# The row maxima take the position bias from SBUF in a combined VectorE instruction

## The chip, the cores and the metric

The kernel runs on one core of a Trainium2 chip. The metric is the device time of one launch in microseconds (us), the median of several runs. An engine named here is one of the core's five: PE is TensorE (matrix products; PEld is its weight load), DVE is VectorE, ACT is ScalarE, POOL is GpSimd, SP is SyncE, which here only issues transfers.

## What is computed

A transformer block over 32 batches of 512 rows of 256 features, with a modulation per batch:

```python
mod = (_silu(L0_c) @ L0_wmod).reshape(L0_c.shape[0], 6, 1, -1)
h = _layernorm(x, axis=-1) * (1 + ca) + sa
x = x + ga * attention(h)
h = _layernorm(x, axis=-1) * (1 + cb) + sb
x = x + gb * ffn(h)
```

The attention has 16 heads of 16 features. Its scores get a bias that depends on the head and on the distance of query and key alone, in 32 buckets that are full beyond a distance of 64 and are constant for keys ahead of the query:

```python
scores = jnp.einsum('bhqd,bhkd->bhqk', q * scale, k)
scores = scores + position_bias * 8.0
attn = softmax(scores)
```

The feed-forward part quantizes its input, its weights and its hidden values (704 wide) to a 4-bit format in blocks of 16, with products in full precision between them.

## The kernel before, in words

**Setup** (to about 98 us of the span) loads and quantizes the weights and builds the bias tables. Then a software pipeline runs over the batches, `for n` from -2 to 32, of which 4 to 29 are a hardware loop over pairs of iterations. An iteration has 16 steps `s` of four places `j`; four steps are a tile of 128 rows of the output, so that an iteration has 4 tiles and 64 places. Each engine has its own program, written out by hand in that same order, and engines meet at semaphores. A table (`JOBS`) says at which place TensorE makes which product of the projections, of the output projection and of the feed-forward part; they use two PSUM banks in turn (`ps_x`), so a job waits until the reader of the job two before it has read.

**Scores** are made twice. `scores` (L593 to L596) makes them with keys on the partitions, for ScalarE to take the exponential of two heads at once (L790) and for `weigh` (L630) to sum the values with. The softmax needs the maximum of each row first, and it has to be there before these scores are made, since it is subtracted through an additional row of `q_rows`. So `maxima` (L609 to L612), one iteration ahead, makes the scores with queries on the partitions, 128 queries by 512 keys in a PSUM bank, and `reduce_max` on VectorE (L1018) takes the negated maximum over the keys into `neg_max`. There is one such pair at each place: 64 in a batch, 2048 in all. The two engines share three PSUM banks for it (`RING_M`): TensorE may write the bank for maximum m once VectorE has read m - 3.

**The bias.** Constant parts of it ride in rows of `q_rows` and `k_rows`. What is left is a band around the diagonal. It is added on TensorE by a second matmul into the same bank, of the reversing matrix `rev` with `band_m` (in fp16): 192 columns wide, or 128 for the first query block (j = 0), which is one in four. `scores` adds its own band in the same manner from `band_t` (L594, L596).

**VectorE** also has, between these maxima, the low parts of high and low splits (`low_of`, L1063; `low_of_hidden`, L1071), the residual sums (`add_attention`, L1083 and L1086; `add_ffn`), statistics and scales (L1094 to L1105, `block_scales` L1053 to L1057), the activation (`silu_times_up`, L1115 and L1121) and the division by the softmax sum (L1047). Its queue is in order: whatever stands ahead of a maximum delays the bank that TensorE waits for. In a tile the places are written (r, j), with r = s mod 4. The activation of the third chunk of the hidden values stands at (2, 3), `block_scales` of 704 values behind the maximum of (3, 0), and the low part of the context, `ctx_l`, ahead of the maximum of (0, 1); ScalarE must first have copied its high part `ctx_h` (L863), and TensorE waits for `ctx_l` with the output projection at (0, 3).

After 32 maxima TensorE transposes them (L680), ScalarE copies them as bf16 into `max_rows` (L858), and a transfer puts them in place in `q_rows`.

## Time and profile before

| | |
|---|---|
| runs | 3733.33, 3735.27, 3738.55 us; median 3735.27 |
| the profiled execution | 3743.46 us, its span 3741.6 us |
| busy in the span | PE 3432.3 (92%), PEld 2016.3 (54%), DVE 2807.5 (75%), ACT 2128.2 (57%), POOL 1711.9 (46%) us |
| mean granted TensorE clock | 0.974 of full speed |
| transfers | mean 63 GB/s, 31.4% of the 16 DMA engines' time |
| the chain that ended last | PE 69%, ACT 10%, issue 7%, DVE 5%, DMA 4% of the span |

Times in the profile are us unless ns is written; an instruction that starts before the one ahead of it has ended overlaps it in the pipeline, so what an instruction costs its engine is the distance of two starts and not its duration. "[0.54 <-PE ...]" at a row's end is idle time of the engine ahead of it and what ended it.

### The profile page before, as it was taken

Reading aid. Unit: us, or ns where it says so; the run is one execution under the profiler, and the core shown is the slowest. Engines: PE = TensorE matmul, PEld = TensorE weight load, DVE = VectorE, ACT = ScalarE, POOL = GpSimd, SP = SyncE. Lnnn points to the kernel's source line nnn. Section 1 sums busy time; section 2 is a strip of 40 time slices with the busy share of each in tenths; the row PEclk is TensorE's granted clock in tenths of the full one; section 3 lists DMA queues with packets and bytes.
Section 4 is the critical chain, followed back from the end, with each engine's and each line's share of the span. In section 5 each row is a group of like instructions: output and inputs, shape, how many; then the busy total and the mean of one; then the engine's idle time right before and its main releaser. Section 6 shows DMA issues by size and latency. Waiting matters only on the chain.

```text
span 3741.6 us, 78263 instructions
## 1 busy us (share of the span) xinstructions
PE 3432.3 (92%) x22910; PEld 2016.3 (54%) x22910; DVE 2807.5 (75%) x5866; ACT 2128.2 (57%) x3352; POOL 1711.9 (46%) x2095
## 2 busy tenths in 40 slices
PE   2599999999999999999999999999999999999986
PEld 1245555555555555555555555555555555555555
DVE  7457877777777777777777777777777877777854
ACT  2256666655666555566655556656556566555552
POOL 2214444444544445454444544444445444444454
PEclk6799999999999999999999999999999999999997
DMA  3553232333323233332323332332333232333000
GB/s 98 84 95 71 52 66 56 60 74 74 69 57 67 48 70 74 73 64 63 64 45 73 76 73 57 61 63 55 73 76 73 51 68 56 61 73 69 18 22 12
DMA packets 199173, 236.95 MB, mean 63 GB/s; under 512 B 23552, under 2 KB 177568, under 8 KB 198736
## 3 DMA queue, kind: packets, MB, share of 16 engines
q1 hardware_dynamic: 198736, 231.51, 31.4%
q8 instruction: 228, 3.74, 0.4%
q14 instruction: 209, 1.71, 0.2%
HBM read 163.59 MB, written 67.31 MB: 62 GB/s over the span
## 4 chain that ended last, share of the span: by engine, by line
PE 69%; ACT 10%; issue 7%; DVE 5%; DMA 4%; SPq 3%; ACTq 1%; POOL 1%; DVEq 0%; POOLq 0%
PE ps_x L641 21%; PE ps_o L630 10%; PE rings L593 10%; PE rings L609 9%; PE ps_x L667 6%; ACT probs L790 5%; DMA x_in<-in_x 3%; PE rings L612 3%; PE rings L594 2%; PE ps_x L674 2%; SPq L484 2%; ACT magic L818 2%; PE rings L596 2%; PE ps_x L706 1%; PE ps_x L685 1%
## 5 line engine op out<-in xcount | busy, mean ns | idle before, releaser
L1018 DVE TENSOR_REDUCE neg_max<-rings 128x1 f32<-128x512 f32 x2048 | 1369.2, 680 | 292.4 <-PE rings L612 265.7
L790 ACT ACTIVATE probs<-rings 128x1024 f32<-128x1024 f32 x1024 | 1050.1, 1025 | 767.7 <-PE rings L596 759.2
L609 PE MATMUL rings<-k_rows,q_rows 120*128 120x512 bf16 x2048 | 779.7, 386 | 24.0 <-DVE neg_max L1018 12.5
L593 PE MATMUL rings<-q_rows,k_rows 121*128 121x512 bf16 x2048 | 727.9, 383 | 73.3 <-ACT probs L790 50.3
L630 PE MATMUL ps_o<-probs,values 128*32 128x512 f32 x4096 | 549.5, 609 | 0.9 <-ACT probs L790 0.9
L612 PE MATMUL rings<-band_m,rev 128*128 128x192 f16 (+1 forms) x2048 | 494.6, 241 | 0.0
L609 PEld LDWEIGHTS rings<-k_rows,q_rows 120*128 120x128 bf16 x2048 | 197.6, 96 | 516.0 <-DVE neg_max L1018 308.4
L594 PE MATMUL rings<-band_t,rev 128*128 128x128 f16 x2048 | 450.4, 220 | 0.0
L1282 POOL TENSOR_TENSOR hidden<-hidden,inv 128x704 f32<-128x704 f32 x128 | 178.6, 1395 | 556.2 <-DVE inv L1057 556.2
L596 PE MATMUL rings<-band_t,rev 128*128 128x128 f16 (+1 forms) x2048 | 431.3, 211 | 0.0
L596 PEld LDWEIGHTS rings<-band_t,rev 128*128 128x128 f16 x2048 | 201.3, 98 | 246.8 <-issue 1.5
L641 PE MATMUL ps_x<-w_gu_h,xq_h 128*128 128x512 f32 (+1 forms) x768 | 323.9, 422 | 10.0 <-DVE hq_l L1071 7.8
L1253 POOL TENSOR_TENSOR hidden<-hidden,magic 128x704 f32<-128x704 f32 x128 | 195.2, 1525 | 281.4 <-ACT magic L820 281.4
L1115 DVE SCALAR_TENSOR_TENSOR tanh<-tanh,ps_x 128x256 f32<-128x256 f32 (+1 forms) x384 | 152.0, 396 | 226.7 <-ACT tanh L877 222.3
L593 PEld LDWEIGHTS rings<-q_rows,k_rows 121*128 121x128 bf16 x2048 | 197.5, 96 | 197.4 <-ACT probs L790 90.2
L641 PE MATMUL ps_x<-w_gu_h,xq_l 128*128 128x512 f32 (+1 forms) x768 | 293.9, 383 | 0.0
L641 PE MATMUL ps_x<-w_gu_l,xq_h 128*128 128x512 f32 (+1 forms) x768 | 291.6, 380 | 0.0
L877 ACT ACTIVATE tanh<-ps_x 128x256 f32<-128x256 f32 (+1 forms) x384 | 138.7, 361 | 197.7 <-PE ps_x L641 197.7
L1063 DVE TENSOR_TENSOR ctx_l<-ps_x,ctx_h 128x256 fp32r<-128x256 f32 x128 | 54.4, 425 | 240.5 <-ACT ctx_h L863 238.9
L641 PE MATMUL ps_x<-w_dn_h,hq_h 128*128 128x256 f32 x768 | 230.2, 300 | 1.5 <-DVE hq_l L1071 1.5
L641 PE MATMUL ps_x<-w_dn_l,hq_h 128*128 128x256 f32 x768 | 219.6, 286 | 0.0
L641 PE MATMUL ps_x<-w_dn_h,hq_l 128*128 128x256 f32 x768 | 219.2, 285 | 0.0
(191 smaller groups left out, 6889.9 us busy)
## 6 DMA issues: line engine op xcount, KB each, us to landing
parts_dram<-parts SPq DMA_DIRECT2D x128, 384.0 KB, 2.3
q_rows<-parts_dram SPq DMA_DIRECT2D x384, 128.0 KB, 4.3
k_rows<-parts_dram SPq DMA_DIRECT2D x384, 128.0 KB, 6.9
mod_rows<-mod_rows_dram SPq DMA_DIRECT2D x32, 640.0 KB, 5.0
x_in<-in_x SPq DMA_DIRECT2D x32, 512.0 KB, 8.7
x_mid<-in_x SPq DMA_DIRECT2D x128, 128.0 KB, 2.1
out<-x_mid SPq DMA_DIRECT2D x128, 128.0 KB, 1.7
probs<-in_wmod SPq DMA_DIRECT2D x1, 1536.0 KB, 7.5
```

What stands on the lines that cost most here:

```text
L593: mm(ps_s[:, bank, :], kr[0:ROW_MAX + 1, h, k0:k0 + P], qr[0:ROW_MAX + 1, h, :], start=True, stop=False)
L594: mm(ps_s[:, bank, k0:k0 + P], rev[:, 0, :], band_t[:, h, :], start=False, stop=False)
L596: mm(ps_s[:, bank, k0 + HALF:k0 + HALF + w], rev[:, 1, :], band_t[:, h, 0:w], start=False, stop=True).then_inc(scores_ready, 1)
L609: mm(ps_m[:, bank, :], q_rows[par][0:ROW_MAX, h, j * P:(j + 1) * P], k_rows[par][0:ROW_MAX, h, :], start=True, stop=False)
L612: mm(ps_m[:, bank, k0:j * P + P], rev[:, 2, :], band_m[:, h, c0:], start=False, stop=True).then_inc(mscores_ready, 1)
L630: m = mm(ps_o[32 * j:32 * j + 32, :], values[:, par, kb, h * VW:h * VW + 32], prob(u, j), start=kb == 0, stop=kb == NT - 1)
L641: m = mm(out, left[a][:, dt, :], right[b][:, dt, columns], start=i == 0, stop=i == len(terms) - 1)
L667: m = mm(ps[:, :], w[:, dt, half * P:(half + 1) * P], h_t[:, dt, :], start=dt == 0, stop=dt == DT - 1)
L790: A(prob_pair(s, j), ps_s, ACT.Exp).then_inc(exp_done, 1)
L1018: v.tensor_reduce(neg_max[:, par, 4 * h + j:4 * h + j + 1], ps_m[:, (4 * h + j) % RING_M, :], AX.X, ALU.max, negate=True).then_inc(max_don ...
L1253: q.tensor_tensor(hid, hid, magic3[:], ALU.add).then_inc(f3_pool.sem, 1)
L1282: q.tensor_tensor(blocks(hid), blocks(hid), spread(inv3[:], FF // BLK), ALU.mult).then_inc(f2_pool.sem, 1)
```

## The change

Five things are different.

- `maxima` on TensorE makes the product of queries and keys alone. The matmul with `band_m` is gone.
- `reduce_max` on VectorE issues a memset of one column, which now carries the wait for TensorE, and then one `tensor_tensor_reduce`: the bank plus 512 columns of `band_z` from SBUF, written back into the bank, with the maximum of the sums in `row_max`. The compiler makes two instructions of it: the pass over 512 columns, and one that writes out the maximum (both print as ISA below).
- `band_z` is a table of fp16, `[128, 320 + 16 x 576]`, zero but for the band of each head; for query block j the instruction reads 512 columns from a start that is 128 j columns further to the left, so that the band comes to lie on the diagonal.
- The setup fills it: a memset of the table, a cast of the Hankel matrix to fp16 into memory that is free then, 8 matmuls of two heads with `rev`, and 16 casts from PSUM, two for each matmul.
- The maximum is no longer negated by VectorE. The ScalarE copy of 32 rows multiplies by -1. The scratch memory for descriptors of the GpSimd DMA is made smaller, for room.

```diff
-        band_m = sb("band_m", [P, H, 3 * HALF], F16)
+        band_z = sb("band_z", [P, 5 * HALF + H * 9 * HALF], F16)
...
+            pe.wait_ge(su_dve, SD["hank"])
+            for i in range(H // 2):
+                if i >= 3:
+                    pe.wait_ge(su_dve, SD["hank"] + 2 * (i - 2))
+                mm(setup_a[:, i % 3, 0:6 * HALF], rev[:, 2, :], hank2_half[:, 2 * i:2 * i + 2, :],
+                   start=True, stop=True).then_inc(su_pe, 1)
...
                 mm(ps_m[:, bank, :], q_rows[par][0:ROW_MAX, h, j * P:(j + 1) * P], k_rows[par][0:ROW_MAX, h, :],
-                   start=True, stop=False)
-                k0, c0 = (0, HALF) if j == 0 else (j * P - HALF, 0)
-                mm(ps_m[:, bank, k0:j * P + P], rev[:, 2, :], band_m[:, h, c0:], start=False,
-                   stop=True).then_inc(mscores_ready, 1)
+                   start=True, stop=True).then_inc(mscores_ready, 1)
...
-                                i = A(max_rows[:], ps[0:32, 0:P], ACT.Copy).then_inc(m_act.sem, 1)
+                                i = A(max_rows[:], ps[0:32, 0:P], ACT.Identity, scale=-1.0).then_inc(m_act.sem, 1)
...
-            step(v.tensor_copy(band_m[:], hank2))
-            step(v.memset(band_m[HALF:P, :, 2 * HALF:3 * HALF], 0.0))
-            step(v.memset(band_m[0:HALF, :, 0:HALF], 0.0))
+            step(v.memset(band_z[:], 0.0))
             dve.wait_ge(su_pe, SP_["wT"])
+            step(v.tensor_copy(hank2_half, hank2))
+            mark("hank")
+            for i in range(H // 2):
+                dve.wait_ge(su_pe, SP_["wT"] + i + 1)
+                rows = setup_a[:, i % 3, 0:6 * HALF].rearrange("p (h n) -> p h n", h=2)
+                heads = slice(2 * i, 2 * i + 2)
+                step(v.tensor_copy(band_m[0:HALF, heads, 0:2 * HALF], rows[0:HALF, :, 0:2 * HALF]))
+                step(v.tensor_copy(band_m[HALF:P, heads, HALF:3 * HALF], rows[HALF:P, :, HALF:3 * HALF]))
...
-                v.tensor_reduce(neg_max[:, par, 4 * h + j:4 * h + j + 1], ps_m[:, (4 * h + j) % RING_M, :], AX.X, ALU.max,
-                                negate=True).then_inc(max_done, 1)
+                v.memset(wait_pad[:, 1 + 4 * h + j:2 + 4 * h + j], 0.0)
+                ps, bias = ps_m[:, (4 * h + j) % RING_M, :], 9 * HALF * h + (6 - 2 * j) * HALF
+                v.tensor_tensor_reduce(ps, ps, band_z[:, bias:bias + S], 1.0, LOWEST, ALU.add, ALU.max,
+                                       row_max[:, par, 4 * h + j:4 * h + j + 1]).then_inc(max_done, 1)
```

On VectorE, from the maximum of (2, 3) to the second instruction behind that of (3, 1), in the part ahead of the hardware loop. Before (`hidden` is the activation, `scale` and `inv` its block scales):

```order
L1121 SCALAR_TENSOR_TENSOR hidden<-tanh,ps_x 128x192
L1018 TENSOR_REDUCE neg_max<-rings 128x1 x2
L1053 TENSOR_REDUCE scale<-hidden 128x44
L1055 TENSOR_SCALAR scale<-scale 128x44
L1057 RECIPROCAL inv<-scale 128x44
L1018 TENSOR_REDUCE neg_max<-rings 128x1
L1103 SCALAR_TENSOR_TENSOR ffn_in<-magic,ffn_in 128x256
L1105 SCALAR_TENSOR_TENSOR ffn_in<-magic,ffn_in 128x256
```

The same stretch now:

```order
L1136 SCALAR_TENSOR_TENSOR hidden<-tanh,ps_x 128x192
L1031 MEMSET wait_pad 128x1
L1033 ISA rings,row_max<-rings,band_z 128x512
L1033 ISA row_max 128x1
L1031 MEMSET wait_pad 128x1
L1033 ISA rings,row_max<-rings,band_z 128x512
L1033 ISA row_max 128x1
L1068 TENSOR_REDUCE scale<-hidden 128x44
L1070 TENSOR_SCALAR scale<-scale 128x44
L1072 RECIPROCAL inv<-scale 128x44
```

Each maximum is three instructions in the place of one; nothing else has moved.

On TensorE at (3, 0) and (3, 1): the maximum's product, the product with the values, the next maximum's product, and the feed-forward part's last product. Before:

```order
L609 MATMUL rings<-k_rows,q_rows 128x512
L612 MATMUL rings<-band_m,rev 128x128
L630 MATMUL ps_o<-probs,values 32x512 x4
L609 MATMUL rings<-k_rows,q_rows 128x512
L612 MATMUL rings<-band_m,rev 128x192
L641 MATMUL ps_x<-w_dn_h,hq_h 128x256
```

Now (rows on semaphores left as they stand):

```order
L619 MATMUL rings<-k_rows,q_rows 128x512
L637 MATMUL ps_o<-probs,values 32x512 x4
L124 REGISTER_ALU
L619 MATMUL rings<-k_rows,q_rows 128x512
L124 ISA x2
L648 MATMUL ps_x<-w_dn_h,hq_h 128x256
```

The band's matmul is gone from behind each product, and the order of the others is the same.

## Rows read from the trace of the kernel before

**Rows 1.** The page's first part: busy time and share of each engine.

```profile
PE 3432.3 (92%) x22910; PEld 2016.3 (54%) x22910; DVE 2807.5 (75%) x5866; ACT 2128.2 (57%) x3352; POOL 1711.9 (46%) x2095
```

**Rows 2.** The page's costliest groups: the maxima on the two engines.

```profile
L1018 DVE TENSOR_REDUCE neg_max<-rings 128x1 f32<-128x512 f32 x2048 | 1369.2, 680 | 292.4 <-PE rings L612 265.7
...
L609 PE MATMUL rings<-k_rows,q_rows 120*128 120x512 bf16 x2048 | 779.7, 386 | 24.0 <-DVE neg_max L1018 12.5
...
L612 PE MATMUL rings<-band_m,rev 128*128 128x192 f16 (+1 forms) x2048 | 494.6, 241 | 0.0
```

**Rows 3.** Busy time in the four tiles of one steady iteration, from `ctx_l` to `ctx_l`.

```profile
core 0: us, PE busy (x) PEld busy (x) DVE busy (x) ACT busy (x) POOL busy (x), PEclk, DMA share, GB/s
1705.90:1734.26 28.36, 27.89 (x187) 16.10 (x184) 21.34 (x43) 19.54 (x33) 12.75 (x18) 1.00 0.05 15
1734.26:1761.61 27.35, 26.37 (x174) 15.07 (x174) 20.92 (x43) 16.69 (x27) 15.17 (x18) 1.00 0.54 113
1761.61:1786.49 24.88, 23.52 (x170) 14.00 (x171) 20.47 (x43) 14.49 (x24) 13.96 (x17) 1.00 0.14 49
1786.49:1814.68 28.19, 27.19 (x187) 16.79 (x185) 21.67 (x52) 14.86 (x24) 11.13 (x16) 1.00 0.52 84
sum 108.78, PE 104.97 PEld 61.95 DVE 84.40 ACT 65.57 POOL 53.01; mean PE 26.24 PEld 15.49 DVE 21.10 ACT 16.39 POOL 13.25
```

**Rows 4.** TensorE's timeline: the band's matmul and what starts behind it.

```profile
1771.67 0.22 PE L612 MATMUL rings<-band_m,rev 128*128 128x128 f16 x1
1771.73 0.39 PE L706 MATMUL ps_x<-ident,hidden 128*128 128x128 f32 x2
...
1775.86 0.39 PE L609 MATMUL rings<-k_rows,q_rows 120*128 120x512 bf16 x1
1776.09 0.25 PE L612 MATMUL rings<-band_m,rev 128*128 128x192 f16 x1
1776.18 0.38 PE L593 MATMUL rings<-q_rows,k_rows 121*128 121x512 bf16 x1
```

**Rows 5.** VectorE's timeline where the first batch's maxima run alone.

```profile
168.04 7.26 DVE L1018 TENSOR_REDUCE neg_max<-rings 128x1 f32<-128x512 f32 x12 [1.33 <-PE rings L612]
```

**Rows 6.** VectorE's groups by shape, near kin of the new instructions.

```profile
L1071 DVE TENSOR_TENSOR hq_l<-ps_x,hq_h 128x512 fp32r<-128x512 f32 x128 | 88.1, 688 | 14.7 <-ACT hq_h L881 14.4
L1063 DVE TENSOR_TENSOR ctx_l<-ps_x,ctx_h 128x256 fp32r<-128x256 f32 x128 | 54.4, 425 | 240.5 <-ACT ctx_h L863 238.9
L1097 DVE BATCH_NORM_AGGREGATE mean_var<-stats 128x2 f32<-128x6 f32 x128 | 22.7, 177 | 5.4
L1096 DVE MEMSET wait_pad<- 128x1 f32 x128 | 7.6, 59 | 0.0
```

**Rows 7.** VectorE's timeline in the shortest tile.

```profile
1766.97 0.42 DVE L1115 SCALAR_TENSOR_TENSOR tanh<-tanh,ps_x 128x256 f32<-128x256 f32 x1 [1.28 <-ACT tanh L877]
...
1771.89 0.42 DVE L1115 SCALAR_TENSOR_TENSOR tanh<-tanh,ps_x 128x256 f32<-128x256 f32 x1 [0.96 <-ACT tanh L877]
...
1783.73 1.27 DVE L1018 TENSOR_REDUCE neg_max<-rings 128x1 f32<-128x512 f32 x2
1786.49 0.43 DVE L1063 TENSOR_TENSOR ctx_l<-ps_x,ctx_h 128x256 fp32r<-128x256 f32 x1 [1.49 <-ACT ctx_h L863]
```

**Rows 8.** TensorE's timeline: the maximum of (0, 3) in the same tile.

```profile
1786.38 0.38 PE L609 MATMUL rings<-k_rows,q_rows 120*128 120x512 bf16 x1
```

**Rows 9.** VectorE's timeline at the end of the setup; the last row is its cast by shape.

```profile
84.57 1.76 DVE L991 CAST band_m<-k_rows 128x3072 f16<-128x3072 f32 x1
86.50 0.48 DVE L992 MEMSET band_m<- 64x512 uint32 x1 [0.17 <-DVE band_m L991]
...
87.67 8.88 DVE L996 CAST k_rows<-x_mid 32x8192 bf16<-32x8192 f32 x2
96.58 1.41 DVE L1028 BATCH_NORM_STATS2 stats<-x_in 128x6 f32<-128x256 f32 x4
...
L968 DVE CAST w_o_h<-hidden 128x512 fp32r<-128x512 f32 x1 | 0.4, 428 | 0.0
```

More of the change, by code:

```diff
@@ L53 @@
 EPS = 1e-5
+LOWEST = -3.0e38
 VW = HD + 1
@@ L283, in build @@
         floor = sb("floor", [P, 1])
-        wait_pad = sb("wait_pad", [P, 1])
+        wait_pad = sb("wait_pad", [P, 1 + H * NT])
         stats, mean_var, rstd = sb("stats", [P, NT, 6]), sb("mean_var", [P, NT, 2]), sb("rstd", [P, NT])
@@ L287, in build @@
         stats2, mean_var2, rstd2 = sb("stats2", [P, 6]), sb("mean_var2", [P, 2]), sb("rstd2", [P, 1])
-        neg_max = sb("neg_max", [P, 2, H * NT])
+        row_max = sb("row_max", [P, 2, H * NT])
         max_rows = sb("max_rows", [32, P], BF16)
@@ L381, in build @@
         hank1 = wm[:, 0:H * P].rearrange("p (h n) -> p h n", h=H)
+        band_m = band_z[:, 5 * HALF:].rearrange("p (h n) -> p h n", h=H)[:, :, 0:3 * HALF]
         hank2 = nrm[:, 0:H * 3 * HALF].rearrange("p (h n) -> p h n", h=H)
+        hank2_half = k_rows[0][:].rearrange("p h s -> p (h s)").bitcast(F16)[:, 0:H * 3 * HALF].rearrange(
+            "p (h n) -> p h n", h=H)
         NG = 2 * FT * D
@@ L679, in job @@
                     wait(pe, max_done, (n + shift) * 64 + 32 * (half + 1))
-                    m = tr(ps[0:32, 0:P], neg_max[:, (par + shift) % 2, 32 * half:32 * half + 32], ident[:])
+                    m = tr(ps[0:32, 0:P], row_max[:, (par + shift) % 2, 32 * half:32 * half + 32], ident[:])
                 elif kind == "oT":
@@ L1030, in layer_norm_1 @@
                     after(dve, a_dve, unit, "st3")
-                    v.memset(wait_pad[:], 0.0)
+                    v.memset(wait_pad[:, 0:1], 0.0)
                     for t in range(NT):
@@ L1095, in ln2_and_fp4 @@
                     after(dve, f1_dve, u, "st")
-                    v.memset(wait_pad[:], 0.0)
+                    v.memset(wait_pad[:, 0:1], 0.0)
                     v.bn_aggr(mean_var2[:], stats2[:]).then_inc(f1_dve.sem, 1)
@@ L1295 @@
 SD = {"silu": 2, "inv0": 6, "inv1": 9, "bo": 10, "mrow": 26, "round0": 31, "round1": 35, "lo": 51,
-      "end": 51 + 4 * DT + FT + 7 + 2}
+      "hank": 51 + 4 * DT + FT + 6, "end": 51 + 4 * DT + FT + 6 + H + 2}
 SO = {"div0": 4, "wq0": 6, "wq1": 7, "end": 7}
@@ L1316 @@
     }
-    nc = bacc.Bacc("TRN2", target_bir_lowering=False, num_devices=1)
+    nc = bacc.Bacc("TRN2", target_bir_lowering=False, num_devices=1, dynamic_dma_scratch_size=2048)
     aps = [nc.dram_tensor(f"in_{n}", arrays[n].shape, F32, kind="ExternalInput").ap() for n in _INS]
```

## Prediction

> **What bounds the kernel now.** I read the busy times first. TensorE is busy for 92% of the span, VectorE for 75% [rows 1], so TensorE is the first suspect; the reader should also see that VectorE has no great reserve. The costliest groups say where the change bites: 2048 reductions of 680 ns are half of VectorE's work, and 2048 band matmuls of 241 ns look like 495 us of TensorE's [rows 2]. That last figure is not what they cost, since matmuls overlap; the timeline decides below. Then I cut one steady iteration into its four tiles [rows 3]. They last 28.36, 27.35, 24.88 and 28.19 us, 108.78 together. TensorE is busy for all but 0.47, 0.98, 1.36 and 1.00 us of them, at the full clock (1.00, the 2.4 GHz level). VectorE is idle for 7.02, 6.43, 4.41 and 6.52 us. The third tile is the shortest because no projection falls in it, while VectorE has about the same work in each: this is the tile in which VectorE is nearest to being the bound.
>
> **What TensorE saves.** A band matmul of 192 columns starts 0.09 us ahead of the next matmul, one of 128 columns 0.06 us [rows 4]. That is its price, also with its weight load, since the next product starts on time. In a tile there are 12 of the wide and 4 of the narrow ones: 12 x 0.09 + 4 x 0.06 = 1.32 us. Over the kernel, 1536 x 0.09 + 512 x 0.06 = 169 us, 4.5% of the time. This is the most that the change can bring.
>
> **What VectorE pays.** Twelve reductions in a row end after 7.26 us, so one costs (7.26 - 0.68) / 11 = 0.60 us of the engine [rows 2, 5], and 0.08 us of its 0.68 overlap the next one. In its place come three instructions.
> - The pass over 512 columns with two inputs, one in PSUM. The nearest row is the two-input subtraction over 512 columns from PSUM and SBUF: 688 ns against 680 [rows 2, 6]. I add 0.01 us. No row shows VectorE writing into PSUM, nor an fp16 input of this kind; I take no more for them, and the rival below prices it.
> - The memset, 59 ns for one column [rows 6]. It costs between nothing, if it slips into the overlap, and 0.06 us. I take 0.06.
> - The write-out of the maximum. No row shows it. The nearest ones are the memset (59 ns) and the statistics' last step over six inputs (177 ns) [rows 6]. It may also have to wait until the pass has left the pipeline, 0.08 us. So it costs 0.06 to 0.26 us; I take 0.11, nearer to the memset, which like it has one output column and no stream to read.
>
> Together 0.18 us on each maximum, which I call d; the ends are 0.06 (one short instruction, the other hidden) and 0.33. VectorE's work grows by 2048 x 0.18 = 369 us, to about 3190 us or 87% of the new span. The Trainium skill, Vector Engine (DVE) Microarchitecture Reference, section "Measured stream behaviour on trn2", gives about 75 ns for each VectorE instruction beside its 1.04 ns per column; the reductions here agree, with 0.60 us for 512 columns. By that rule two more instructions give d = 0.15, an estimate, and the sum below would end near 3629 us and not 3639.
>
> **A tile with projections** (the first, second and fourth) has 6.4 us or more of idle VectorE time against 16 x 0.18 = 2.9 us. What VectorE waits for there are products and their copies, so it takes the additional work into its waits. TensorE's 1.32 us then come off the tile, less what other waits of TensorE keep (it stands idle for 0.5 to 1.0 us in such a tile [rows 3]). I take 1.1 us.
>
> **The third tile** has to be followed. VectorE waits for the activation's tanh for 1.28 us and then for 0.96 us [rows 7]. The first wait has four maxima ahead of it: 4 x 0.18 = 0.72, and TensorE arrives 0.33 earlier, together below 1.28. The second has three more: 0.54 + 0.27, below 0.96. Both waits stay, so at 1771.89 VectorE is still paced by TensorE, and is earlier by the 7 band matmuls between, 0.6 us. From there it works without a pause up to 1785.00, through nine maxima, and then waits for 1.49 us for `ctx_h` before `ctx_l` [rows 7]. Nine times 0.18 is 1.62 us: the wait is gone and VectorE is 0.13 us late by its old schedule, less the 0.6. So the tile becomes shorter by 0.47 us and not by 1.1. The same is seen on the ring of banks: TensorE's product of (0, 3) starts at 1786.38 [rows 8] and needs the bank whose maximum was read at 1785.00, 1.38 us before; nine maxima later by 1.62 and TensorE earlier by some 0.75 use this up, so TensorE is held there, for about the 0.85 us that the tile doesn't gain. What is late next, behind `ctx_l`, is the output projection at (0, 3), which waits for it.
>
> **Sum for the steady part.** 3 x 1.1 + 0.47 = 3.77 us for each iteration. There are 32 batches of 64 maxima; those of the first run alone ahead of the others. 31 x 3.77 = 117 us gained.
>
> **The start.** The first batch's maxima run one behind the other on VectorE [rows 5], with TensorE waiting for banks. Of its 64, those of 14 heads fall into the iteration that has no scores yet: 56 x 0.18 = 10 us. The end of the setup is a serial stretch on VectorE: the cast, two memsets, the casts of `k_rows`, then the first batch's statistics [rows 9]. The cast stays in another form. The two memsets go, 1.3 us from the cast's end to 87.67. In come a memset of 4768 words, at 0.48 us for 512 of them 4.5 us; 16 casts of 64 partitions by 256 columns, each at most the 0.43 us of a cast of 512 columns and at least half, so 0.36 with the semaphore, 6 us; and about 1 us until the first matmul's result is there. Net 11 us (7 to 14), all on the path. The 64 copies by ScalarE with the factor -1 cost nothing: a copy is an activation before and after, and ScalarE is busy for 57% of the span.
>
> Net: 117 - 10 - 11 = 96 us gained. The profiled execution took 3743.5 us, so 3647.5; it stands 8.2 us above the median of the runs, and against that median the forecast is **3639 us**, 2.6% less.
>
> **Rivals.**
>
> *VectorE becomes the bound.* The three instructions don't overlap at all: 0.08 for the pass's tail, 0.06, 0.18, and 0.10 for the tail and hand-over of the small ones, d = 0.42. The place is every tile. VectorE then needs 84.40 + 64 x 0.42 + 2 (half a microsecond of wait left in each tile) = 113.3 us for an iteration in place of 108.78: 31 x 4.5 = 140, with 11 and 24 for the start 175 us more, 3910 us. It decides from about d = 0.33 on: at 64 x 0.33 = 21.1 an iteration is 1.3 us shorter than before, of which the start takes back all but 10 us in the whole kernel; at 0.37 it is 72 us slower, 3807. For it: three instructions for one, on an engine that in the third tile has 4.41 us of reserve. Against it: the one short instruction of this kind in the trace takes 59 ns [rows 6]. The Trainium skill, VectorE: DVE Perf Modes, section "Rules for kernel authors", speaks for this rival: it advises to keep the number of VectorE instructions small, since each empties the pipeline. Chance 0.19.
>
> *The bank.* If reading and writing one PSUM bank take turns, the pass costs 0.53 us more, d = 0.71, and an iteration 84.40 + 45.4 + 2 = 131.8 us: 31 x 23.0 + 11 + 40 = 764 us more, about 4500. Nothing in the trace shows VectorE writing PSUM, so no row excludes it; reads from PSUM with a second input from SBUF run at full pace, 425 ns for 256 columns [rows 6]. Chance 0.04.
>
> *The relief doesn't arrive.* TensorE comes earlier but finds the banks or `ctx_l` no earlier in any tile, and only the start's 21 us show: about 3756, or nothing measurable if a little arrives. Against it: the idle time of VectorE in three tiles. Chance 0.11.
>
> That the change doesn't do what it says is excluded for TensorE by the order of its instructions, in which the band's matmul is gone.
>
> **How the numbers follow.** The forecast's case, d from 0.06 to 0.33, has 0.66, all of it faster. At d = 0.06 every tile gains its 1.32 us: 31 x 5.3 - 11 - 3 = 150 us, some 3585; a little of it is always lost, so the range starts at 3590. It reaches up to d = 0.37, 3805 us, which leaves out half of the first rival and all of the second, and 0.05 below: 0.18 in all. What a measurement can tell from no change is about 0.2%, 7.5 us. The third rival gives 0.06 to "same" and 0.05 to "slower". Slower: 0.19 + 0.04 + 0.05 = 0.28.
>
> **What would show it.** In the changed kernel's profile the pass should last 0.68 to 0.70 us, and from the memset's start to the next instruction behind the write-out should take 0.78 us when VectorE is not waiting. VectorE busy near 87%, TensorE's share no lower than 90%. The tiles by `ctx_l`: 27.3, 26.3, 24.4 and 27.1 us. VectorE's wait for `ctx_h` should be gone in the third tile and remain in the others. The first statistics should start near 107.5 us and not at 96.58. I am wrong if d is over 0.33, if the first, second and fourth tiles don't shorten by a microsecond, or if TensorE waits for banks outside the third tile.

## The result: 33 us less, where 96 were forecast

The kernel before took 3735.18 us (median of 4 runs, 3733.33 to 3738.55), the changed one 3701.99 us (median of 4 runs, 3699.32 to 3706.56). The ratio is 0.991, 95% interval 0.9897 to 0.9923. The change is a gain of 0.9%; the direction was right, the size was a third of the forecast.

### The profile page after: what moved, and what is told of

It reads as the page before. It is cut to its first block, busy times and chain, and to the rows that moved or that the text cites. A ratio compares the mean times of both kernels' runs of the same rounds, so it can differ in the third digit from the quotient of the medians.

```text
span 3700.5 us, 78302 instructions
## 1 busy us (share of the span) xinstructions
PE 3294.8 (89%) x20870; PEld 1927.5 (52%) x20870; DVE 2937.5 (79%) x9977; ACT 2135.1 (58%) x3352; POOL 1705.9 (46%) x2095
## 4 chain that ended last, share of the span: by engine, by line
issue 48%; POOL 30%; PE 10%; DVE 5%; ACT 3%; POOLq 2%; DMA 2%; SPq 1%; ACTq 0%; DVEq 0%
POOL hidden L1270 4%; POOL hidden L1268 4%; POOL hidden L1297 4%; PE ps_x L648 4%; POOL parts L1236 3%; POOL proj L1229 3%; POOL ffn_in L1285 2%; POOL rstd L1280 2%; POOL x_mid L1263 2%; PE rings L603 1%; PE ps_o L637 1%; POOL hidden L1272 1%; POOLq L124 1%; POOL ffn_in L1301 1%; PE ps_x L674 1%
## 5 line engine op out<-in xcount | busy, mean ns | idle before, releaser
L1033 DVE CUSTOM_DVE_ANT_0 rings<-rings,band_z 128x512 f32<-128x512 f32 x2048 | 1408.4, 698 | 168.1 <-issue 165.4
L619 PE MATMUL rings<-k_rows,q_rows 120*128 120x512 bf16 x2048 | 768.4, 387 | 38.1 <-DVE row_max L1033 28.7
L603 PE MATMUL rings<-q_rows,k_rows 121*128 121x512 bf16 x2048 | 728.3, 383 | 80.9 <-ACT probs L797 67.1
L648 PE MATMUL ps_x<-w_gu_h,xq_h 128*128 128x512 f32 (+1 forms) x768 | 351.8, 458 | 20.1 <-DVE hq_l L1086 17.8
L606 PEld LDWEIGHTS rings<-band_t,rev 128*128 128x128 f16 x2048 | 201.6, 98 | 246.9 <-issue 1.8
L1033 DVE DVE_READ_ACCUMULATOR2_ANT row_max<- 128x1 f32 x2048 | 287.0, 140 | 0.0
L648 PE MATMUL ps_x<-w_dn_h,hq_h 128*128 128x256 f32 x768 | 242.5, 316 | 1.5 <-DVE hq_l L1086 1.5
L604 PEld LDWEIGHTS rings<-band_t,rev 128*128 128x128 f16 x2048 | 202.0, 99 | 46.1 <-issue 20.2
```

The source lines that it names most:

```text
L603: mm(ps_s[:, bank, :], kr[0:ROW_MAX + 1, h, k0:k0 + P], qr[0:ROW_MAX + 1, h, :], start=True, stop=False)
L604: mm(ps_s[:, bank, k0:k0 + P], rev[:, 0, :], band_t[:, h, :], start=False, stop=False)
L606: mm(ps_s[:, bank, k0 + HALF:k0 + HALF + w], rev[:, 1, :], band_t[:, h, 0:w], start=False, stop=True).then_inc(scores_ready, 1)
L619: mm(ps_m[:, bank, :], q_rows[par][0:ROW_MAX, h, j * P:(j + 1) * P], k_rows[par][0:ROW_MAX, h, :], start=True, stop=True).then_inc(mscores ...
L648: m = mm(out, left[a][:, dt, :], right[b][:, dt, columns], start=i == 0, stop=i == len(terms) - 1)
L1033: v.tensor_tensor_reduce(ps, ps, band_z[:, bias:bias + S], 1.0, LOWEST, ALU.add, ALU.max, row_max[:, par, 4 * h + j:4 * h + j + 1]).then_i ...
```

## The profile after

The page's first part of the changed kernel, for [rows 1]:

```profile
span 3700.5 us, 78302 instructions
...
PE 3294.8 (89%) x20870; PEld 1927.5 (52%) x20870; DVE 2937.5 (79%) x9977; ACT 2135.1 (58%) x3352; POOL 1705.9 (46%) x2095
```

TensorE has 137.5 us of work less, so its relief is real. VectorE has 130 us more, not the 369 of the forecast, and half of these 130 are not the maxima (next rows). The span is shorter by 41 us only, so TensorE now waits more.

VectorE's groups by shape, for [rows 2, 6], first of the changed kernel, then the one row of before that turned out to matter:

```profile
L1033 DVE CUSTOM_DVE_ANT_0 rings<-rings,band_z 128x512 f32<-128x512 f32 x2048 | 1408.4, 698 | 168.1 <-issue 165.4
L1033 DVE DVE_READ_ACCUMULATOR2_ANT row_max<- 128x1 f32 x2048 | 287.0, 140 | 0.0
L1101 DVE TENSOR_TENSOR x_mid<-exp,x_mid 128x256 f32<-128x256 f32 x128 | 184.5, 1441 | 6.0
...
L1031 DVE MEMSET wait_pad<- 128x1 f32 x2048 | 120.8, 59 | 63.7 <-PE rings L619 53.6 <-issue 10.2
```

```profile
L1086 DVE TENSOR_TENSOR x_mid<-exp,x_mid 128x256 f32<-128x256 f32 x128 | 118.0, 922 | 6.1
```

The pass lasts 698 ns, inside the 0.68 to 0.70 that I gave it. The third row is a surprise: an instruction that the change doesn't touch, the residual sum of `add_attention`, went from 922 to 1441 ns, which is 66 of VectorE's 130 us. Its rows are long (over 0.7 us) 64 times of 128 before and 121 times now.

Four tiles of one steady iteration of the changed kernel, cut at `ctx_l` as in [rows 3], with the same columns:

```profile
1582.41:1610.49 28.08, 26.72 (x169) 15.44 (x168) 21.69 (x75) 19.64 (x33) 12.78 (x18) 1.00 0.05 16
1610.49:1637.87 27.38, 25.72 (x159) 14.48 (x159) 22.56 (x76) 16.80 (x27) 15.16 (x18) 1.00 0.55 97
1637.87:1663.27 25.40, 22.07 (x153) 13.13 (x153) 22.05 (x76) 14.74 (x24) 14.14 (x17) 1.00 0.22 75
1663.27:1690.85 27.58, 26.31 (x170) 16.16 (x170) 22.91 (x87) 14.67 (x24) 10.61 (x16) 1.00 0.52 79
sum 108.44, PE 100.82 PEld 59.21 DVE 89.21 ACT 65.86 POOL 52.70; mean PE 25.20 PEld 14.80 DVE 22.30 ACT 16.47 POOL 13.17
```

TensorE is busy for 4.15 us less than in [rows 3], and the iteration is hardly shorter. Its idle time in the four tiles was 0.47, 0.98, 1.36 and 1.00 us and is 1.36, 1.66, 3.33 and 1.27 us. The second tile, with 1.66 us of it, is as long as before.

The third and the fourth tile trade time with each other from one iteration to the next, in both kernels (25.40 and 27.58 here, 23.96 and 29.60 in the next one), so one iteration is a poor sample. The table below has means over 12 or 13 consecutive iterations (about 1100 to 2500 us of the span), from the starts of `ctx_l` on VectorE's timeline. The choice of the stretch moves the mean of an iteration by some 0.1 us, nearly all of it in tiles 3 and 4, so the columns of tiles 1 and 2 are the firm ones. The ratio is of whole runs; the kernel before ran again beside each group of runs, with medians between 3732.2 and 3739.8 us, so that differences of ratios, times 3735, are safer than differences of the times themselves. "Tiles 3+4" is their sum.

| kernel | tile 1 | tile 2 | tiles 3+4 | iteration | ratio to before, 95% interval |
|---|---|---|---|---|---|
| before | 28.36 | 27.34 | 54.02 | 109.72 | 1 |
| the changed kernel | 28.09 | 27.37 | 52.97 | 108.42 | 0.991 [0.9897, 0.9923] |
| pe_only | 27.89 | 26.81 | 52.66 | 107.36 | 0.9807 [0.9791, 0.9823] |
| dve_only | 28.86 | 27.78 | 54.24 | 110.88 | 1.0083 [1.0066, 1.01] |
| noport_before | 28.34 | 27.34 | 54.06 | 109.74 | 1.0005 [0.9995, 1.0015] |
| nudge2_before | 28.33 | 27.55 | 53.82 | 109.69 | 1.0017 [1.0007, 1.0026] |
| noport_dve_only | 28.59 | 27.46 | 53.96 | 110.00 | 1.0031 [1.002, 1.0043] |
| noport_after | 27.79 | 26.90 | 52.66 | 107.34 | 0.9841 [0.9824, 0.9857] |
| late_before | 28.34 | 27.34 | 53.41 | 109.09 | 0.9977 [0.9965, 0.9989] |
| late_after | 27.73 | 26.85 | 52.32 | 106.91 | 0.9814 [0.9797, 0.983] |
| late_noport_after | 27.43 | 26.36 | 52.32 | 106.11 | 0.9755 [0.9738, 0.9771] |
| late_pe_only | 27.45 | 26.30 | 52.04 | 105.80 | 0.9693 [0.9677, 0.971] |
| late_noport_pe_only | 27.28 | 26.34 | 52.03 | 105.65 | 0.9688 [0.9672, 0.9704] |

The first two rows tell the result's sum: 1.30 us for each iteration, 31 x 1.30 = 40 us, less the start, which took 10 us more (below), is 30; 33 were measured. Over all 31 iterations, from the first `ctx_l` to the 125th, it is 3347.9 us before and 3297.9 now, 50 us less; the first `ctx_l` comes 8.7 us later, which leaves the 41 us between the two profiled spans (the profiled execution of the kernel before was 8 us above its median). The iteration that the prediction was worked on, 108.78 us, is 0.94 us shorter than the mean of the table's stretch and 0.78 us longer than the mean of all 31, 108.00.

The end of the setup in the changed kernel, on VectorE's timeline, for [rows 9] (16 casts in all):

```profile
83.84 4.03 DVE L998 MEMSET band_z<- 128x4768 uint32 x1 [1.06 <-issue]
87.90 1.76 DVE L1000 CAST k_rows<-k_rows 128x3072 f16<-128x3072 f32 x1
90.33 0.42 DVE L1006 CAST band_z<-rings 64x256 f16<-64x256 f32 x1 [0.67 <-PE rings L587]
...
97.17 0.43 DVE L1007 CAST band_z<-rings 64x256 f16<-64x256 f32 x1
97.63 8.88 DVE L1009 CAST k_rows<-x_mid 32x8192 bf16<-32x8192 f32 x2
106.55 1.40 DVE L1043 BATCH_NORM_STATS2 stats<-x_in 128x6 f32<-128x256 f32 x4
```

The statistics start at 106.55 and not at 96.58: 10.0 us, for 11 forecast.

## Where the time stops: two places in the second tile

I follow the second tile, which kept its whole length. First VectorE behind its start, then GpSimd, in the kernel before (the tile starts at 1734.26):

```profile
1737.17 0.42 DVE L1086 TENSOR_TENSOR x_mid<-exp,x_mid 128x256 f32<-128x256 f32 x1
...
1739.07 0.42 DVE L1115 SCALAR_TENSOR_TENSOR tanh<-tanh,ps_x 128x256 f32<-128x256 f32 x1 [0.88 <-ACT tanh L877]
...
1741.03 0.18 DVE L1097 BATCH_NORM_AGGREGATE mean_var<-stats 128x2 f32<-128x6 f32 x1
...
1737.24 1.60 POOL L1257 TENSOR_TENSOR hidden<-hidden,scale 128x704 f32<-128x704 f32 x1
```

The same in the changed kernel (the tile starts at 1610.49):

```profile
1613.51 1.63 DVE L1101 TENSOR_TENSOR x_mid<-exp,x_mid 128x256 f32<-128x256 f32 x1
...
1615.69 0.41 DVE L1130 SCALAR_TENSOR_TENSOR tanh<-tanh,ps_x 128x256 f32<-128x256 f32 x1
...
1617.66 0.18 DVE L1112 BATCH_NORM_AGGREGATE mean_var<-stats 128x2 f32<-128x6 f32 x1
...
1613.47 1.39 POOL L1272 TENSOR_TENSOR hidden<-hidden,scale 128x704 f32<-128x704 f32 x1
```

**The hold.** The sum has both inputs in SBUF. Before, it starts 2.91 us into the tile, 0.07 ahead of GpSimd's product, and takes 0.42 us. Now it starts 3.02 us into the tile, 0.04 behind GpSimd's product, and its row ends at 1615.14, after that product's end at 1614.86: 1.63 us. The three maxima in between cost the 0.11 us that make the difference, and 0.11 us late becomes 1.3. The Trainium skill, SBUF — State Buffer, section "Who interferes with whom", states that a VectorE instruction with two SBUF inputs contends with a GpSimd instruction that reads SBUF, that the shared port pair is an exclusive lock, and that the order of issue decides who blocks. The trace agrees: 0.42 us when the sum starts first, 1.63 when the product does. What becomes of the 1.21 us is seen two rows on: VectorE had waited 0.88 us for ScalarE's tanh, that wait is gone, and the aggregate that the statistics end with starts 7.17 us into the tile and not 6.77. From it GpSimd makes `shift`, for which ScalarE waits with `ffn_in`, and the tanh of the next chunk stands behind that in ScalarE's queue. On ScalarE before, then in the changed kernel:

```profile
1742.65 0.60 ACT L809 ACTIVATE ffn_in<-x_mid,shift,rstd 128x256 f32<-128x256 f32 x1 [0.94 <-POOL shift L1268]
...
1743.68 0.36 ACT L877 ACTIVATE tanh<-ps_x 128x256 f32<-128x256 f32 x1
```

```profile
1619.28 0.60 ACT L816 ACTIVATE ffn_in<-x_mid,shift,rstd 128x256 f32<-128x256 f32 x1 [1.52 <-POOL shift L1283]
...
1620.31 0.36 ACT L884 ACTIVATE tanh<-ps_x 128x256 f32<-128x256 f32 x1
```

The tanh starts 9.42 us into the tile before and 9.82 now, and VectorE waits for it in both. So all that VectorE does from there is 0.40 us late.

**The gate.** The next place is (2, 3), where TensorE makes a projection's product into the PSUM bank whose reader is the low part `hq_l` of the job two before. Before, on VectorE and then on TensorE:

```profile
1746.68 0.41 DVE L1053 TENSOR_REDUCE scale<-ffn_in 128x16 f32<-128x256 f32 x1
...
1747.52 0.42 DVE L1071 TENSOR_TENSOR hq_l<-ps_x,hq_h 128x256 fp32r<-128x256 f32 x1
...
1748.28 1.48 PE L667 MATMUL ps_x<-h_t,w_q 128*128 128x512 f32 x3
```

The changed kernel:

```profile
1623.34 0.42 DVE L1068 TENSOR_REDUCE scale<-ffn_in 128x16 f32<-128x256 f32 x1
...
1624.18 0.42 DVE L1086 TENSOR_TENSOR hq_l<-ps_x,hq_h 128x256 fp32r<-128x256 f32 x1
...
1624.74 1.55 PE L674 MATMUL ps_x<-h_t,w_q 128*128 128x512 f32 x3 [0.27 <-DVE hq_l L1086]
```

Before, `hq_l` ends at 1747.94, 13.68 us into the tile, and the product starts at 14.02: 0.34 us to spare. Where the product does wait, it starts 0.14 us behind the end of `hq_l`, so 0.20 of the 0.34 are what TensorE may gain here before it waits, beyond what `hq_l` itself gains. Now `hq_l` ends at 14.11 and the product starts at 14.25, later than before although TensorE has done some ten band matmuls less by then. `hq_l` stands in VectorE's queue behind the three small instructions of the block scales (0.84 us, from 1623.34 to 1624.18), by the written order alone; they work on something else, the feed-forward input of the next tile.

TensorE's waits for `hq_l` with the three projections, from the table of waits. Of before, then of the changed kernel:

```profile
PE ps_x L674 <- DVE hq_l L1071: 4.3, 14, 0.4
```

```profile
PE ps_x L667 <- DVE hq_l L1086: 7.4, 28, 0.3
PE ps_x L674 <- DVE hq_l L1086: 7.1, 28, 0.3
PE ps_x L681 <- DVE hq_l L1086: 7.0, 28, 0.3
```

Each of the three projections waits 28 times, where before one did, 14 times.

Other waits of TensorE grew too, and the gate has no part in them. In the same table its waits for ScalarE's exponentials (`probs`) went from 50.3 to 67.1 us.

## The experiments

Three theories stand against each other: TensorE's saving is real but stops at the gate; the port hold eats it; VectorE's additional work d for each maximum eats it, as the prediction's main rival had it. The gate theory was made only after the first four runs (pe_only, dve_only and the two of noport). In the expectations of those four, theory 1 is the hold, theory 2 the price of VectorE's instructions, and theory 3 that the band's matmul is hardly on the path.

**The change taken apart.** pe_only removes the band's matmul and puts nothing in its place. The band is left out of the row maxima only; the scores that the softmax uses keep it, and what is subtracted there is then near the maximum, not the maximum itself.

```diff
-                   start=True, stop=False)
-                k0, c0 = (0, HALF) if j == 0 else (j * P - HALF, 0)
-                mm(ps_m[:, bank, k0:j * P + P], rev[:, 2, :], band_m[:, h, c0:], start=False,
-                   stop=True).then_inc(mscores_ready, 1)
+                   start=True, stop=True).then_inc(mscores_ready, 1)
```

> The kernel before, with the band's matmul taken away and nothing put in its place: the maxima are taken without the band (the output only needs some bound of each row there). VectorE's work is as before. Theory 1 (the gain was lost because VectorE reaches the residual sum x_mid 0.1 us later in each tile, just after a GpSimd instruction has started, and is held by it for 1.2 us; this delays a loop through GpSimd, ScalarE and TensorE): here the sum starts 2.9 us behind ctx_l as before and mostly stays at 0.42 us, and about 1 us comes off each tile with projections: 3610 us, 3590 to 3640. Theory 2 (VectorE's three instructions are simply too dear, and TensorE waits for its banks): 3580 to 3600, nearly all of 169 us. Theory 3 (the band's matmul is hardly on the path, whatever VectorE does): 3700.

Measured: 3665.82 us against 3739.8, ratio 0.9807, 74 us less. That is under half of the 169 us that the band matmuls cost TensorE by their pitch, with VectorE at 2803 us of work, as before. None of the three expected ranges holds it: it is 26 us above theory 1's, and the residual sum starts 2.91 us into the second tile, as before, so in that tile the hold is not what keeps the gain away; it is 66 us above theory 2's and 34 below theory 3's time. So most of the loss is there without any new work on VectorE, and a place that no theory had yet named keeps it. The gate in its second tile (start 1696.60):

```profile
1709.73 0.42 DVE L1068 TENSOR_TENSOR hq_l<-ps_x,hq_h 128x256 fp32r<-128x256 f32 x1
...
1710.30 1.55 PE L664 MATMUL ps_x<-h_t,w_q 128*128 128x512 f32 x3 [0.24 <-DVE hq_l L1068]
```

The product starts 13.70 us into the tile, 0.32 earlier than before, and TensorE has waited for it: 0.20 is the spare time less the hand-over, and the rest is that `hq_l` ends 0.13 us earlier, at 13.55.

dve_only keeps the band on TensorE and adds the three instructions, with a table of zeros as the second input. ScalarE's copy negates as in the change, and a memset of the zeros (0.27 us) joins the setup.

```diff
-                v.tensor_reduce(neg_max[:, par, 4 * h + j:4 * h + j + 1], ps_m[:, (4 * h + j) % RING_M, :], AX.X, ALU.max,
-                                negate=True).then_inc(max_done, 1)
+                v.memset(wait_pad[:, 1 + 4 * h + j:2 + 4 * h + j], 0.0)
+                ps = ps_m[:, (4 * h + j) % RING_M, :]
+                v.tensor_tensor_reduce(ps, ps, nothing[:], 1.0, LOWEST, ALU.add, ALU.max,
+                                       neg_max[:, par, 4 * h + j:4 * h + j + 1]).then_inc(max_done, 1)
```

> The kernel before with its band's matmul kept, and VectorE's part of the change alone: memset, combined instruction with a row of 512 zeros in fp16 from SBUF, write-out. The output stays the reference's. Theory 1: the residual sum starts about 0.1 us later behind ctx_l and takes 1.4 us in the mean in place of 0.92, the loop is longer in the tiles that had been free of this: 3760 to 3790 us. Theory 2: each maximum costs 0.1 us or more and TensorE waits for banks: above 3800. Theory 3: within 5 us of 3735.

Measured: 3769.66 us, ratio 1.0083, 30 us more; the residual sum takes 1505 ns. That is in theory 1's range. The parts add up: -74 + 30 and 10 for the setup, which neither of them has, is -34, and the change has -33; each part is known to some 6 us. But 30 us is not d: the three maxima ahead of the sum cost 0.11 us more, 0.037 each, or 2048 x 0.037 = 76 us of VectorE's time, part of which falls into its waits.

**The hold.** In noport the gated projection is written back into its own PSUM bank and the sum reads it from there, so that it has one input in SBUF. The bank is then released after the sum and not before it.

```diff
-                    "ctxT": (f1_dve, "ctxl"), "wo": (f1_dve, "ga"), "xqT": (f2_dve, "xql"), "g0": (f2_dve, "h0"),
+                    "ctxT": (f1_dve, "ctxl"), "wo": (f1_dve, "res"), "xqT": (f2_dve, "xql"), "g0": (f2_dve, "h0"),
...
-                v.tensor_tensor(exp2[:], ps[:, 0:D], mod_rows[:, rp, 0, :], ALU.mult).then_inc(f1_dve.sem, 1)
+                v.tensor_tensor(ps[:, 0:D], ps[:, 0:D], mod_rows[:, rp, 0, :], ALU.mult).then_inc(f1_dve.sem, 1)
...
-                v.tensor_tensor(x_mid[:, t, :], exp2[:], x_mid[:, t, :], ALU.add).then_inc(f1_dve.sem, 1)
+                v.tensor_tensor(x_mid[:, t, :], ps[:, 0:D], x_mid[:, t, :], ALU.add).then_inc(f1_dve.sem, 1)
```

> The changed kernel, with the gated projection written back into its PSUM bank and the residual sum x_mid reading it there: that sum then has one input in SBUF and not two; the bank is released after the sum and not before it. Theory 1: the sum takes 0.42 us in every tile and GpSimd no longer holds it, the loop is 1.2 us shorter: 3610 to 3650 us. Theories 2 and 3: 3700, within 8.

> The kernel before with the same move of that product into PSUM. The sum was held in 46 of 100 tiles (mean 0.92 us). Theory 1: those tiles get shorter where TensorE is not the bound, the first one above all: 3700 to 3725 us. Theories 2 and 3: 3735, within 5.

Measured, noport_after: 3679.22 us, ratio 0.9841 against the change's 0.991, 26 us less; that lies between theory 1's 3610 to 3650 and the others' 3700, so the hold is real and is not the whole loss. Its sum, by shape:

```profile
L1101 DVE TENSOR_TENSOR x_mid<-ps_x,x_mid 128x256 f32<-128x256 f32 x128 | 54.4, 425 | 6.1
```

425 ns, in all of 128. noport_before: 3740.56 us, ratio 1.0005, nothing, although 64 of the 128 sums of the kernel before were held, nearly all of the first tile's among them. So a hold costs little in the kernel before, and theory 1 missed here.

The reverse shows it from the other side: a memset of a scratch tile ahead of `add_attention`'s reading of the projection makes the sum late in the kernel before. nudge_before has 100 columns (142 ns), nudge2_before 200 (225 ns).

```diff
+        nudge = sb("nudge", [P, 200])
...
+                v.memset(nudge[:], 0.0)
                 ps = read_job(it, s - 1, "wo")
```

> The kernel before, with a memset of 100 columns (0.1 us) on VectorE ahead of the two instructions of the residual sum at (1, 0), 128 times, 13 us in all. It makes the sum start 0.1 us later behind ctx_l, as the changed kernel does. If the start by GpSimd in those 0.1 us is what decides: the sum's mean goes from 0.92 to 1.4 us or more, and the time rises by more than the memsets' own 13 us, to 3755 to 3780. If it is the delay itself: at most 3748, and the sum's mean stays near 0.92.

Measured: 3742.74 us, ratio 1.0007 [0.9997, 1.0016]. Inconclusive: the sum moved only to 2.97 us behind the tile's start and won its race; its mean fell to 806 ns.

> As nudge_before, with a memset of 200 columns. The first one moved the sum by 0.06 us only, to 2.97 us behind ctx_l, just ahead of GpSimd's third instruction at 2.98, and neither the sum nor the time changed. This one moves it to about 3.07 us. If the start by GpSimd decides, the sum's mean goes from 0.92 us to 1.4 or more, and with it the time to 3755 to 3775, of which at most 25 us are the memsets themselves. If not, the mean stays near 0.92 us and the time within 3740 to 3752.

Measured: 3736.62 us, ratio 1.0017. The sum now starts 3.07 us into the tile and is held 122 times of 128 (mean 1436 ns). In the same second tile:

```profile
1730.87 1.57 DVE L1088 TENSOR_TENSOR x_mid<-exp,x_mid 128x256 f32<-128x256 f32 x1
```

So the order of the two starts does decide the hold, but 4 to 6 us (3 to 10 by the interval) is all that it costs together with the memset, and my 3755 to 3775 were a miss. The port theory, with a hold that costs the same everywhere, fell here: in the kernel before, VectorE's 0.88 us of wait for tanh take most of a hold. The second tile is 0.21 us longer and the third and fourth 0.20 shorter.

The last run asks whether the same hold is dear once the maxima are slower: noport_dve_only has the edits of dve_only and of noport together.

> The kernel before with the combined VectorE instruction added and the band kept on TensorE, as in dve_only (1.0083 of the kernel before), and the attention's residual sum now reads its gated projection from PSUM, so that it can't be held by GpSimd. Theory A (the hold is cheap while VectorE has slack, as nudge2_before showed, and expensive once each maximum takes longer): the sum falls from 1.5 to about 0.4 us and 15 to 28 us of dve_only's +30 go, ratio 1.001 to 1.004. Theory B (the +30 are the 0.04 us more of each maximum through VectorE's chains, the hold costs as little as in nudge2_before): ratio 1.006 to 1.008, at most 8 us less than dve_only. In both the maximum's pass stays 698 ns, and the setup's 2 us memset and the maxima of the first batch stay in the total.

Measured: 3747.66 us, ratio 1.0031. Of dve_only's 0.83% the hold is 0.52%, about 19 us; the remaining 12 us are d (the memset of the zeros is 0.27 us, not the 2 of the expectation). That is that run's theory A. The price of the hold is 0 to 6 us where VectorE's maxima have their old length, and 19 to 26 us where each takes 0.037 us more.

The first tile shows why. Its sum is held in the kernel before too (1.51 us). What covers a hold is VectorE's next wait, for tanh. Without a hold, in the runs of noport, that wait is 0.86 us in the kernel before, 0.64 with dve_only's maxima and 0.52 in the changed kernel (medians of 15 iterations). With the hold, VectorE reaches tanh later by 0.15, 0.28 and 0.31 us, and the first tile is longer by 0.02, 0.27 and 0.30 us. In the second tile the cover is exceeded in nudge2_before too: 1.15 us of hold and 0.16 of memset against 0.88, and `hq_l` is 0.35 us late. There TensorE's 0.20 us of spare time take part of it; in the changed kernel TensorE has used them up. How the third and fourth tile make up for the rest was not followed.

**The gate.** In late, the block scales of the feed-forward input move from (2, 1) to (2, 2), where they stand behind `hq_l`. The computation is the same.

```diff
-                if at == (2, 1):
+                if at == (2, 2):
                     after(dve, f1_pool, u, "add")
                     block_scales(
```

> The kernel before, with VectorE's block scales of the feed-forward input (three instructions, 0.85 us) moved from (2, 1), where they stand ahead of the low part hql1, to (2, 2) behind it. Theory now (gate theory): the product that TensorE makes at (2, 3) in three of four tiles waits for hql1, the reader of the job two before it; in the kernel before that was ready 0.34 us ahead of its use, so moving it forward gives nothing: 3735, within 8. Rival (VectorE's load as such paces the tiles, wherever its work stands): also 3735. This run is the control of the next two.

Measured: 3731.17 us, ratio 0.9977: 9 us. Before the change the gate is hardly ever closed in the first two tiles, which stay as they are; the gain is all in tiles 3 and 4, 0.61 us.

> The same move in the kernel whose maxima have no band at all (pe_only, 3666). There TensorE arrives at (2, 3) 0.68 us earlier and the product starts 0.46 us late, because hql1 ends at 13.53 us behind ctx_l as before. Gate theory: that product starts on time, and 0.4 to 0.7 us come off each of three tiles: 3600 to 3630. Rival (load): 3666, within 6. Third possibility: the next gate in the row, ScalarE's six operations from the k projection to ctx_h, takes over at once: 3640 to 3660.

Measured: 3624.39 us, ratio 0.9693, 43 us less than pe_only (0.0114 of 3735). The gate is worth five times as much once TensorE is ahead of it. Tiles 3 and 4 gain 0.62 us, as in late_before; what is new are the 0.44 and 0.51 us of the first two.

> The same move in the changed kernel (3702). VectorE reaches hql1 at 13.69 us behind ctx_l there and TensorE waits for it for 0.27 us in the tile looked at. Gate theory: 3640 to 3675. Rival (load): 3702, within 6.

Measured: 3668.73 us, ratio 0.9814, 36 us less than the change. VectorE and TensorE at (2, 3) in its second tile (start 1705.29):

```profile
1718.13 0.42 DVE L1086 TENSOR_TENSOR hq_l<-ps_x,hq_h 128x256 fp32r<-128x256 f32 x1
...
1719.09 0.41 DVE L1068 TENSOR_REDUCE scale<-ffn_in 128x16 f32<-128x256 f32 x1
...
1719.11 1.88 PE L674 MATMUL ps_x<-h_t,w_q 128*128 128x512 f32 x4
```

`hq_l` ends 13.26 us into the tile, the product starts at 13.82 with no wait, and the table of waits has no row of a projection for `hq_l` any more. The product starts 0.43 us earlier than in the change (14.25), and the second tile is 26.85 us and not 27.37. The first two tiles gain 0.36 and 0.52 us, where late_before had nothing.

**Both.** Two kernels have late and noport together, on the change and on pe_only.

> The changed kernel with both cures: the block scales behind hql1, and the residual sum reading its product from PSUM. If the two losses are separate, their gains (33 and 23 us) add up: 3645. If both relieve the same gate at (2, 3), the second gives less: 3655 to 3668.

Measured: 3639.95 us, ratio 0.9755. The gate alone gave 0.0096, the port alone 0.0069, both give 0.0155: they nearly add, and my alternative that both relieve the same place (3655 to 3668) is out. With both, the change brings 92 us, close to the forecast's 96. That is luck: the prediction's own working with a d as small as the measured one would have given some 150.

> The kernel without any band in the maxima, with both cures: the fastest that is expected. The late scales alone gave 3624. The sum is held there in about half of the tiles (mean 0.97 us): 3610 to 3620.

Measured: 3615.84 us, ratio 0.9688, the fastest of all, and within the interval of late_pe_only. So with maxima of the old length the hold costs next to nothing (2 us) even when TensorE is relieved; it is the longer maxima that make it dear. This kernel leaves the band out of the row maxima, so it subtracts a value that can lie off the maximum by what the band adds; the setup's 10 us and VectorE's d are saved too. Among the kernels that subtract the maximum itself, late_noport_after is the fastest, 1.6% below the change.

## Why the prediction was right and wrong

- *TensorE saves 1.32 us in a tile.* Its busy time fell by 4.15 us in the iteration shown and by 137.5 us in all, and late_noport_pe_only brings 4.07 of the 5.28 us to the end of an iteration. As an upper bound it was not exceeded; no run tests the 1.32 by itself.
- *d = 0.18, between 0.06 and 0.33.* The pass was right (698 ns). The other two parts were not: the memset slips under the running pass, and the write-out's row of 140 ns overlaps what follows. The last section has the rows. Measured 0.037 in the steady part and 0.05 in an unbroken row of maxima, below my lower end. This error alone would have made the gain larger than forecast: at my own d = 0.06 the working gave 150 us.
- *"A tile with projections ... it takes the additional work into its waits. ... I take 1.1 us."* This is the step that failed, and a gain of less than a microsecond in these tiles was one of my own signs of being wrong. The three such tiles were to gain 1.1 each, 3.3 together. The first two gained 0.27 and lost 0.03 (table). I took VectorE's idle time as a sum, 6.4 us and more, and asked only whether the additional work fits into it. What TensorE waits for is a single instruction of VectorE, `hq_l`, which stood 0.34 us ahead of it. TensorE can be earlier there by that spare time, less 0.14 of hand-over, and by what `hq_l` itself gains; VectorE's idle time does not enter. pe_only shows the step wrong with no new work at all: 2.36 us for an iteration and not 5.28. Moving three instructions out of the way of `hq_l` gives 36 us in the changed kernel.
- *A term that the sum did not have.* The prediction let every other instruction of VectorE last as before. The residual sum went from 922 to 1441 ns, held behind GpSimd, and taking that hold away gives 26 us.
- *The third tile gains 0.47, its wait for `ctx_h` goes.* Wrong in both. In the iterations of the kind that the prediction was worked on, the third tile goes from 24.88 to 23.98 us, 0.90 less, and VectorE's wait for `ctx_h` at its end goes from 1.49 us to 0.64 and not to nothing. In pe_only, where each maximum costs what it did, it is 23.93 us and 0.93. The changed kernel, then pe_only:

```profile
1770.26 0.42 DVE L1078 TENSOR_TENSOR ctx_l<-ps_x,ctx_h 128x256 fp32r<-128x256 f32 x1 [0.64 <-ACT ctx_h L870]
```

```profile
1747.33 0.42 DVE L1060 TENSOR_TENSOR ctx_l<-ps_x,ctx_h 128x256 fp32r<-128x256 f32 x1 [0.93 <-ACT ctx_h L860]
```

  So the nine maxima took some 0.3 us more (an estimate from 0.93 less 0.64), not 1.62, and VectorE never was the bound. In the other iterations, as the one shown above (25.40 us), nothing is waited for at `ctx_l`, because VectorE has waited 2.03 us for TensorE's maximum just ahead of it:

```profile
1662.61 0.06 DVE L1031 MEMSET wait_pad<- 128x1 f32 x1 [2.03 <-PE rings L619]
```

  The third and fourth tile together gained 1.05 of the 1.57 forecast. What divides the time between them was not settled.
- *The start.* 10 us in the first batch's maxima: by the distance in an unbroken row it is 56 x 0.05 = 3. Setup 11 us: 10.0 measured, the memset 4.03 for 4.5, 16 casts 7.3 for 6.
- *VectorE near 87%, TensorE no lower than 90%.* 79% and 89%. (The 3190 us should read 2807.5 + 369 = 3177.)
- *The rivals.* VectorE as the bound needed d = 0.42, the bank 0.71; both fell with the pass's 698 ns and d. The relief that doesn't arrive was the nearest to the truth, though only in part: I had it as TensorE finding the banks and `ctx_l` no earlier, and gave no thought to `hq_l`. TensorE's waits for `ctx_l` with the output projection did grow. Of before, then of the changed kernel:

```profile
PE ps_x L641 <- DVE ctx_l L1063: 39.0, 89, 1.3
```

```profile
PE ps_x L648 <- DVE ctx_l L1078: 62.0, 84, 1.3
```

Those 23 us are relief given back at the end of the tile. They are there in pe_only too (61.5 us) and not in dve_only (38.3), so they come from TensorE being early. The wait for ScalarE's exponentials grew by 17 us, in pe_only by 27. TensorE's waits for the banks of the maxima were 12.5 us (11 times) and are 28.7 (31 times), and 27.3 (35 times) in pe_only, so these don't come from VectorE's new work either. No run took these waits away, so what they would bring is open.

By the iteration, in the table: pe_only -2.36, and -3.92 with late; the other 1.36 of the 5.28 go to waits that no run separated; dve_only +1.16, of which the hold is 0.88 (110.88 - 110.00); together -1.20, and -1.30 measured in the change.

## What to carry to other kernels

When the busiest engine is relieved, list for each of its steps how long its input has been ready, and look first at the smallest. Beyond that lead the engine gains there only what the input itself gains. The idle time of the other engine, taken as a sum, doesn't bound it. The place where it is small is often a queue that holds an unrelated instruction ahead of the needed one, and moving that instruction costs nothing: here it gave 36 us where the change gave 33. And look at what else starts within a tenth of a microsecond of a VectorE instruction with two inputs in SBUF, when GpSimd works on SBUF at the same time.

## What was not expected of the hardware

**Three instructions for 0.04 us more.** VectorE in the changed kernel, two maxima with nothing to wait for:

```profile
162.33 0.70 DVE L1033 CUSTOM_DVE_ANT_0 rings<-rings,band_z 128x512 f32<-128x512 f32 x1
162.36 0.06 DVE L1031 MEMSET wait_pad<- 128x1 f32 x1
162.94 0.14 DVE L1033 DVE_READ_ACCUMULATOR2_ANT row_max<- 128x1 f32 x1
162.95 0.73 DVE L1033 CUSTOM_DVE_ANT_0 rings<-rings,band_z 128x512 f32<-128x512 f32 x1
...
173.50 0.72 DVE L1033 CUSTOM_DVE_ANT_0 rings<-rings,band_z 128x512 f32<-128x512 f32 x1
...
174.15 0.72 DVE L1033 CUSTOM_DVE_ANT_0 rings<-rings,band_z 128x512 f32<-128x512 f32 x1
```

From the first pass to the second it is 0.62 us, for 0.60 of one reduction [rows 5]. The next maximum's memset has its row under the running pass, and the next pass starts 0.01 us behind the write-out's start. When more maxima follow in an unbroken row, the distance is 0.65 us, as in the last two rows. In the steady part, from a pass to the next instruction, it is 0.61 to 0.64 us. The 75 ns for each instruction that the prediction quotes from the Trainium skill, Vector Engine (DVE) Microarchitecture Reference (section "Measured stream behaviour on trn2") would have given 0.15; for short instructions between long ones the measurement decides, 0.037 for two.

**Reading and writing one PSUM bank.** The pass reads 512 columns from a bank and writes them back into it in 698 ns, 18 ns more than a reduction that only reads. The bank rival needed 0.53 us more; there is no sign of it.

**The port.** A sum of 256 columns takes 0.42 us if it starts 0.07 us ahead of a GpSimd product over 704 columns, and 1.63 us if it starts 0.04 behind; over all tiles of the changed kernel 121 of 128 are long. With its first input in PSUM it takes 425 ns at all 128 places.
